# Cross-attention with a top-2 expert layer: the opening's common end removed, its loads and its work laid out anew

## What is computed

```python
# x: 8 x 256 x 256, ctx_2048: 8 x 1601 x 256, itok: 8 x 256 (token -> key number, below 128)
q, kv = layernorm(x), ctx_2048
kv_c = kv @ W_kvc;  q_c = q @ W_dq                       # 64 and 96 columns
q_nope, q_rope = q_c @ W_uq, rope(q_c @ W_qr)            # 16 heads x 128, 16 heads x 64
k_nope, v, k_rope = kv_c @ W_uk, kv_c @ W_uv, rope(kv_c @ W_kr)
scores = (q_nope . k_nope + q_rope . k_rope) * scale
good = (k_ids <= seg_id) & (k_ids >= seg_id - 8)         # only keys 0..127 can be seen
x = x + softmax(where(good, scores, -1e30)) @ v @ W_o
# second layer: x + mean over the two best experts of relu(layernorm(x) @ expert_w[e] + expert_b[e])
```

## Time and profile before

| | us |
|---|---|
| median of 3 runs | 407.98 |
| lowest, highest | 406.57, 410.68 |
| the profiled execution, its own time | 408.24 |
| its span in the profile | 406.4 |
| PE busy in the span | 369.6 |
| DVE, ACT, POOL busy | 292.4, 261.4, 233.2 |

### The profile page before, as it was taken

One profiled execution on the slowest core, in us unless ns is written; L12 is line 12 of the kernel. 1 busy time (PEld: TensorE's weight loads), 2 busy tenths in 40 slices (PEclk: granted clock), 3 DMA queues, 4 the chain that ended last, 5 costly groups with the idle time before them and its releaser, 6 DMA issues.

```text
span 406.4 us, 10417 instructions
## 1 busy us (share of the span) xinstructions
PE 369.6 (91%) x2533; PEld 294.1 (72%) x2533; DVE 292.4 (72%) x1406; ACT 261.4 (64%) x902; POOL 233.2 (57%) x320
## 2 busy tenths in 40 slices
PE   1908799999999999999999999999997989999992
PEld 1804678788888888878887888878885667777661
DVE  2617677687888888888888988888889557444276
ACT  1123587888888778787787878888886435444341
POOL 4013485766767667676677676776763224666600
PEclk9966899999999999999999999999999999999998
DMA  8997000000000000000000000000000414653186
GB/s 236 280 370 209 2 3 1 2 1 2 28 15 15 29 1 26 13 13 26 0 26 26 0 26 0 26 26 0 28 7 22 106 52 129 185 168 118 32 303 232
DMA packets 28551, 28.28 MB, mean 70 GB/s; under 512 B 9308, under 2 KB 26479, under 8 KB 28256
## 3 DMA queue, kind: packets, MB, share of 16 engines
q1 hardware_dynamic: 22672, 19.47, 16.6%
q0 software_dynamic: 2960, 6.94, 4.8%
q10 hardware_dynamic: 2880, 1.43, 1.3%
HBM read 17.81 MB, written 10.91 MB: 71 GB/s over the span
## 4 chain that ended last, share of the span: by engine, by line
PE 63%; issue 11%; DVE 10%; POOL 5%; ACT 2%; DVEq 1%; POOLq 0%; ACTq 0%
PE psum L637 10%; PE psum L1060 10%; PE psum L638 8%; PE psum L639 8%; PE psum L1030 7%; PE psum L1110 5%; PE psum L1052 5%; PE psum L975 3%; POOL prob L1251 2%; POOL q_sb L1233 2%; DVE nsc L1480 2%; PE psum L961 2%; PE psum L564 2%; DVE x_all L1428 1%; PE psum L506 1%
## 5 line engine op out<-in xcount | busy, mean ns | idle before, releaser
L1130 ACT ACTIVATE prob<-nsc,nmax 128x128 f32<-128x128 f32 x256 | 100.8, 396 | 33.6 <-DVE nmax L1480 32.9
L1233 POOL TENSOR_TENSOR q_sb<-rope_a,rope_b 128x256 f32<-128x256 f32 x64 | 47.1, 737 | 69.8 <-DVE rope_b L1453 69.5
L1480 DVE CUSTOM_DVE_ANT_0 nsc<-psum,mask 128x128 f32<-128x128 f32 x256 | 58.9, 285 | 16.7 <-PE psum L1060 16.5
L1251 POOL TENSOR_TENSOR prob<-prob,prec 128x512 f32<-128x512 f32 x64 | 67.4, 1053 | 4.1 <-DVE prec L1459 4.1
L1060 PE MATMUL psum<-kT_all,qT 128*128 (+1 forms) x512 | 68.3, 276 | 0.0
L1060 PEld LDWEIGHTS psum<-kT_all,qT 128*128 128x128 f32 x512 | 62.5, 192 | 0.8 <-ACT qT L1173 0.7
L1295 POOL DMA_INDIRECT halves<-jout,jidx x33 | 32.3, 978 | 30.7 <-issue 14.5
L1130 ACT ACTIVATION_READ_ACCUMULATOR prob<-nsc,nmax 128x1 f32 x256 | 48.4, 189 | 0.0
L1030 PE MATMUL psum<-ident,q_sb 128*128 128x128 f32 x256 | 42.3, 288 | 1.1 <-POOL q_sb L1233 0.3
L637 PE MATMUL psum<-wo_hi,oT_hi 128*128 128x256 f32 x128 | 41.0, 320 | 2.3 <-DVE oT_lo L1440 1.2
L1030 PEld LDWEIGHTS psum<-ident,q_sb 128*128 128x128 f32 x256 | 27.3, 142 | 20.3 <-POOL q_sb L1233 12.2
(11 more groups left out here) (194 smaller groups left out, 889.5 us busy)
## 6 DMA issues: line engine op xcount, KB each, us to landing
wanted<-slots SPq DMA_DIRECT2D x33, 129.0 KB, 2.2
wo_raw<-in_w_o SPq DMA_DIRECT2D x2, 1024.0 KB, 10.9
we_raw<-in_expert_w SPq DMA_DIRECT2D x1, 2048.0 KB, 13.8
half<-halves SPq DMA_DIRECT2D x4, 512.0 KB, 5.1
x_all<-in_x SPq DMA_DIRECT2D x2, 640.0 KB, 7.9
slots<-pad_row SPq DMA_DIRECT2D x8, 129.0 KB, 12.0
ctxT<-in_ctx_t SPq DMA_DIRECT2D x2, 512.0 KB, 5.8
out<-x_all SPq DMA_DIRECT2D x2, 512.0 KB, 5.3
```

The lines of the kernel that those rows point to most:

```text
L1130: e = act.activation(prob[r][:, h, :], nsc[r][:, h, :], ACT.Exp, bias=nmax[r][:, h:h + 1], scale=-1.0, accum_out=psum_h[r][:, h:h + 1])
L1233: pool.tensor_tensor(q_sb[1 - r][:, :, KVC:P], rope_a[1 - r][:], rope_b[1 - r][:], ALU.add).then_inc(m["rope_joined"], 1)
L1251: pool.tensor_tensor(p[:], p[:], prec[1 - r][:, :].unsqueeze(2).to_broadcast([P, HG, P]), ALU.mult).then_inc(m["prob_normed"], 1)
L1480: e = dve.tensor_tensor_reduce(nsc[r][:, h, :], B_S[r][:, h, :], mask[(k // GPT) % 2][:], -SCALE, BIG, ALU.add, ALU.min, nmax[r][:, h:h + 1])
```

## The change

- **One block.** The opening's lists stand at the head of each engine's list of the main block. There is no common end; new waits say what each step needs (`kT_sb`, `wq_lo_done`, `kcat_done`, `qc_sb`, `wg_done`, `before16_done`, `counted`, `flag_done` and others).
- **Layouts.** The host hands over W_kvc, W_dq, W_uq, W_uk, W_uv, W_o and the near context rows so that each partition's part is one piece: W_uq was pieces of 384 bytes and is one of 6 KB per partition, `ctxT` was pieces of 512 bytes and is one of 8 KB. `ctxT` now lies in the memory of `we_raw`.
- **Loads.** SP's order is x of batch 0, W_uq, W_uk, query rope, context, W_uv, W_o first half, x part 1, W_o second half, gate bias, x parts 2 and 3. The expert weights are issued after the second half of the keys is made, the expert bias after DVE's small splits (slot 3), the eight stores to `slots` after those.
- **Order of work.** PE does the query fold in two halves around the latents of batch 0. Keys of batches 0 to 3 are made in slot -2 and turned in slot -1, those of 4 to 7 made in slot 0 and turned in slot 1. Output folds 0, 1 and 2, 3 stand in slots 0, 1, 1 and 2. Statistics go batch by batch (`batch_stats`, slots 0 to 6 for batches 1 to 7, with one `batch_rstd` on POOL each); norm and turn of batch n stand in slot n and its latents in slot n + 1. The expert splits move to slots 7 to 14 (ACT) and 8 to 15 (POOL). POOL's constants move to slot -2 and DVE's small splits to slot 3.

```diff
-        prep = prep_only.enter_context(nc.Block())
...
+        def late_loads(sp, ctx_read):
+            sp.wait_ge(S(ctx_read), 2 if ctx_read == "k_mm" else 16)
+            sp.dma_start(we_raw[:], expert_w.rearrange("(c p) n -> p c n", p=P)).then_inc(S("ld_we"), 16)
+            sp.wait_ge(S("eb_step"), 3)
+            for r in range(2):
+                sp.dma_start(bias2[r:r + 1, :].bitcast(F32), eb2[:, r, :].bitcast(F32)).then_inc(S("ld_bias"), 16)
...
+            pe.wait_ge(S("ld_wuq"), 32)
+            fold_q(0)
+            pe.wait_ge(S("ld_wdq"), 16)
+            pe.wait_ge(S("xT_sb"), 1)
...
+            fold_q(1)
...
+                if isinstance(i, int) and i == -2:
+                    keys(pe, 0)
                 if isinstance(i, int) and i == -1:
-                    fold_o(pe, 0)
-                    fold_o(pe, 1)
+                    key_turn(pe, 0)
...
+                if isinstance(i, int) and i == 0:
+                    keys(pe, 1)
+                    fold_o(pe, 0)
+                if isinstance(i, int) and i == 1:
+                    key_turn(pe, 1)
+                    fold_o(pe, 1)
                     fold_o(pe, 2)
+                if isinstance(i, int) and i == 2:
                     fold_o(pe, 3)
...
-                if piece_of(i - 1, EXPERT_PIECES):
-                    we_low(pool, i - 1)
+                if piece_of(i - 8, EXPERT_PIECES):
+                    we_low(pool, i - 8)
...
+                if piece_of(i - 1, B - 1):
+                    x_norm(dve, i)
...
+                if piece_of(i, B - 1):
+                    batch_stats(dve, i + 1)
```

558 lines of the change are left out of this document (302 added, 256 removed).

## The result

Median 404.66 us (403.12 to 408.19, 20 runs) against 410.61 us for the kernel before on the same chip (405.44 to 411.82, 20 runs); the ratio is 0.990, 95% interval 0.9873 to 0.9927, so about 1% less time. The ratio counts all runs, and those of the kernel before lie in two groups (seven from 405.4 to 408.1, thirteen from 410.0 to 411.8), so it isn't the quotient of the two medians, 0.986. The forecast was 399.5 us, 8.5 less than before. The profiled execution took 403.49 us (span 401.7) against 408.24 (span 406.4): 4.75 us less, so a little over half of what was forecast. The absolute number lies in the range given, and still the sum was wrong: about half of the gain is missing.

A forecast was written before the change was run, and what follows sets the result against it. PE, busy 91% of the span, was taken as the bound past some 50 us. A 12.2 us lead at slot 9, less 1.0 (DVE), 2.0 (POOL) and 0.7 (clock), gave 8.5 us earlier: 399.5 us, 8-in-10 range 394.5 to 405.

The forecast's parts named there:

- the sum: Whole kernel: lead of 12.2 us at slot 9, less 1.0 for DVE, 2.0 for POOL, 0.7 for clock: 8.5 us earlier.
- The hole and its price: Opening: PE stands idle 10.47 us until 31.71, while SP issues eight stores until 29.4 and the common end falls at 29.8.
- Until the scores of slot 0: Opening up to slot 0's scores: PE's list shortens, so they start at 22.8 us instead of 40.82, 18.0 us earlier.
- Slots 0 to 3: Work taken out of the opening returns and PE waits for DVE's chain; the lead shrinks from 18.0 to 13.6 us.
- DVE in slots 1 to 6 and one turn and one set of latents more: Slots 1 to 9: late score steps on DVE cost 1.0 us (bounds 0 and 5), PE's extra turn and latents 1.4.
- rival B: Slots 1 to 8: DVE's chain is the bound, leaving a gain of about 3 us, so 405 us; chance 0.15.
- POOL in slots 8 to 15: Expert splits of 1.27 us fall in slots of 4.06; 16.8 us of work in 16.24 costs 2.0 us (bounds 0, 5).
- Clock: Slots -1 to 3: many short gaps make at least one fall of PE's clock likely; 0.7 us taken, bounds 0 to 6.
- Rival A: Whole kernel: POOL and DVE are no bounds, costs of 1.0, 2.0 and 0.7 fall away; 395.8 us; chance 0.17.
- Rival C: Opening and slots 0 to 5: PE never leaves its lower clock level; slower than before, up to 412 us; chance 0.04.
- Rival D: Opening: SP's large pieces starve ACT's small loads, PE starts 3 us later; 402.5 us; chance 0.10.
- I leave it at 8.36: Opening: PE's first wait, for the third load of ACT's queue, was taken to end at 8.36 us as before.

The follow-up runs named there:

- the second execution of the same kernel: The kernel after, unchanged, run and profiled again beside others on the same chip; ratio 0.9918 to the kernel before.
- the eight variants: Eight edits of the kernel after: POOL's expert splits moved or left out, or steps of slots 1 or 2 reordered, alone or combined; ratios 0.9798 to 0.9954.
- the earlier splits: Kernel after with expert splits four slots earlier (ACT in slots 3 to 10, POOL in 4 to 11); median 406.19 us, ratio 0.9954 to the kernel before.

## Why the prediction was right or wrong, by its own steps

**Where the 4.0 us went.** The sum gave a lead of 8.5 us, measured are 4.5. By slot 9 1.7 are missing (9.5 for 11.2). The splits on POOL cost 4.3 where 2.0 were taken, 2.3 more. Another 0.6 are lost behind slot 9 without any split, where the sum has nothing. Against that, the 0.7 that the sum took off for the clock at its end lie, where they fell, in the 1.7 already.

**The hole and its price: right.** The 10.47 us of idle time end with SP's list, as the earlier trace rows read: moving the stores alone brought PE's start forward by 6.6 us and gave 8.3 of lead.

**Until the scores of slot 0: right to 0.9 us** (23.66 for 22.8). The second fold half ends and the keys begin at 16.74 (forecast 16.9); the fold's first half at the lower clock took 2.82 us, 1.4 more than half of 2.74, as was set for it, and its second 1.69. That the clock came back just between the halves was luck: in the second execution of the same kernel the second half took 2.57, and in the eight variants 1.50 to 2.56. Keys done at 18.7, forecast 18.5. The waits for `kcat` and the join were there (1.00 and 0.81). The turn of the queries began at 21.92 (forecast 21.55). Behind it the clock fell, granted 0.50 from about 22.4 to 25.9 us: the three products took 1.33 us from start to start (0.92 at full clock in slot 1), so some 0.4 of the 0.9 are the clock's, and the scores of slot 0 ran at half speed.

```profile
22.00:23.00 1.00, 1.00 (x6) 0.91 (x7) 0.00 (x0) 0.38 (x1) 0.29 (x1) 0.72 1.10 348
23.00:24.00 1.00, 1.00 (x5) 0.79 (x4) 0.10 (x1) 0.21 (x1) 0.00 (x0) 0.50 1.05 332
```

**Slots 0 to 3: right mechanism, 2.3 us too little** (lead 11.3 for 13.6, 0.9 of it brought from slot 0). The chain named for slot 2 is the one that PE waits for (`qT` by ACT, 1.23 us), at 38.83 for "near 37". The other term is slot 3: `latent_sb` "ends near 42.5, scores at 43.8" was 44.76 and 46.12. The norm of x took 1.13 us beside the join (0.72 was counted on), the four score steps came behind it, then exponentials, `wo_high`, `wo_low` and only then the copy. Two of these steps in another order gave 1.4 us back. So 5.9 us were given back in slots 0 to 3, where the sum has 4.4.

**DVE in slots 1 to 6 and one turn and one set of latents more: 2.4 forecast, 1.8 measured** (slot 4 to 9). Slots 3 to 5 took 5.20 to 5.21 us with PE busy throughout, and DVE up to 5.14 (forecast: above 90% in slots 1 to 6; in slots 1 to 5 it was 80, 82, 99, 98 and 88%, the first two being stretched by PE's waits):

```profile
46.12:51.33 5.21, 5.21 (x40) 4.24 (x39) 5.14 (x27) 3.61 (x12) 3.57 (x5) 1.00 0.02 5
51.33:56.53 5.20, 5.20 (x39) 4.23 (x38) 5.10 (x23) 3.94 (x15) 2.51 (x3) 1.00 0.52 164
```

So rival B, DVE's chain as the bound of slots 1 to 8 at a price of some 9 us, is refuted from slot 3 on: DVE was busy for 99 and 98% of slots 3 and 4, and PE didn't wait. In slots 1 and 2 DVE and ACT do hold PE, as the forecast itself had it. What the Trainium skill says of the shared interfaces ("GPSIMD Engine Reference", Specifications) agrees with the duration of the norm here (1.13 us beside the join in slot 2, 0.72 without) and, with this slack, says nothing of the time.

**POOL in slots 8 to 15: the step that failed.** It was put at "I take 2.0", "slots 12 to 15 lose at least 0.6 us", from a sum of work against the slot's length. By leaving the splits out it is 4.3 us, within the bounds given (0 and 5). And the reason was wrong: with the same sum of work, placed last, about 1.1 us are lost. The check named for it failed too. "POOL above 95% in slots 12 to 15" was this, in the windows of the three slots 12 to 14 (the fifth busy time is POOL's):

```profile
91.56:107.71 16.15, 13.33 (x96) 10.28 (x96) 14.72 (x57) 12.15 (x43) 12.83 (x16) 1.00 0.05 17
```

POOL was busy for 79%, and 1.7 us of its idle time were waits for DVE's rotation, one of them behind the step that was held. POOL was treated as a bucket, where it is a list in which PE's two results, norm and join, stand behind what is put ahead of them. "In slot 12 the two indirect stores and their wait stand between the split and the next join" had the place and gave it no price. What was not seen at all is that DVE is held through the whole of a POOL run without gaps. The prediction knew of the hold and priced it as if it were one instruction of DVE against one of POOL, and only for the norm of x. The hold itself is not new: in the kernel before a step of the same group (`gt`, L1332) took 1.14 us at the median of its 16 instances, for 0.22 alone. With a split in the run it is 2.85 us. How much of the 4.3 us is the hold and how much the later norm and join is not separated by any run.

**Clock: 0.7 forecast.** The clock line was misread: 0.68 and 0.65 in slices 3 and 4 of the kernel before mean the lower level for 64 and 70% of them, not "some 40%"; no term of the sum hangs on it. In the profiled pair it cost 0.95 us in slot 0 (6.17 us; 5.22 in the second execution of the same kernel). But it also moves the medians. Executions whose clock falls behind slot 63 have tails of 94.8 to 96.6 us, those without it 93.2 to 93.5, and both kinds occur with the same program. How often may differ by kernel: nine of the twelve runs of the earlier splits had a clock of 0.985 or lower, and four of the twenty runs of the kernel after had 0.984. Why is not shown.

**The others.** Rival A (no cost by POOL and DVE, 395.8 us) is refuted by the splits' 4.3 us. Rival C did not come. Rival D: in the ten profiles of the kernel after and its variants PE starts at 8.50 to 9.57 us, in the four with the old layouts at 6.61 to 8.36. That is 1.6 us on the mean, over half of the rival's 3, of which the profiled pair shows 0.3; "I leave it at 8.36" holds for that pair only. In the kernel before with all layouts new it was 9.67 and 11.69. The loads behind the first were in time, as counted: no wait of PE from 9 to 90 us is for a DMA. Slots past 16 have kept their length but for 0.6 us in slots 16 and 17.

## What to carry to other kernels

Before pricing a large rearrangement, price its smallest part: here one statement moved past a common end gave 8.3 us of lead, the whole change 4.5. When a step is added to an engine that others wait for, don't add up its work; write down what of the others' is behind it in its list, and put it behind that. (That was worth 3.3 us here for splits in slots 8 to 15; with splits in slots 4 to 11 the last place cost too.) And compare kernels at a mark ahead of any fall of the clock (here the scores of slot 63), or medians will credit or blame the edit for it.
